# Capsule routing rounds 2 to 6 as one stream: norms in six pieces inside the stream, softmax per 16 places, at least one chunk per bucket

## The chip, the cores and the metric

The kernel runs on one core of one Trainium2 chip. The metric is the device time of one execution in microseconds. The core has five engines that run beside each other and wait for each other through semaphores: TensorE (PE, matmuls; PEld is its weight load), VectorE (DVE), ScalarE (ACT), GpSimd (POOL) and SyncE (SP), which here only issues DMAs. The host's work is not in the time.

## What is computed

A residual network of four graph layers over 6250 nodes with 128 features and 106250 edges, each followed by a layer norm. The change is in the fourth layer, a routing over capsules: a node's 128 features are 8 capsules of 16. The reference, cut to that layer:

```python
def _L3_gnn_ref(x, edge_index):
    K, NITER, TAU, EPS = 8, 6, 1.0, 1e-12
    def _factor_normalize(v):
        nrm = jnp.linalg.norm(v, axis=-1, keepdims=True)
        return v / jnp.maximum(nrm, EPS)
    n, d = x.shape
    k, dd = (K, d // K)
    src, trg = (edge_index[0], edge_index[1])
    xk = _factor_normalize(x.reshape(n, k, dd))
    z = xk[src]
    u = xk
    for _ in range(NITER):
        p = jax.nn.softmax(jnp.sum(z * u[trg], axis=2) / TAU, axis=1)
        msg = (z * p[:, :, None]).reshape(-1, d)
        agg = jax.ops.segment_sum(msg, trg, num_segments=n)
        u = _factor_normalize(agg.reshape(n, k, dd) + xk)
    return u.reshape(n, d)
...
x = _layernorm(x + _L3_gnn_ref(x, edge_index), axis=-1)
```

The edges hold both directions of 50000 drawn pairs and one self loop per node. The edge list is an input, so the order of the work for it is made on the chip.

## The kernel before

Nodes lie in 49 tiles of 128 (NT; NTP = 50 with a spare one). The edges are sorted by the tile of their target, a bucket, and each bucket is cut into chunks of 128 edges, one edge per partition. Two chunks of one bucket make a pair. The program has room for 464 pairs (NPAIR); a table, pair_tile, tells each pair's bucket at run time, and pair_at where its data lie in DRAM. A bucket's last pair may have an empty half, which the flags in pair_ok set to zero.

The first round (`first_round`) gathers z for each edge with indirect DMAs and stores it in zo_tab, beside the bytes of two 128 x 128 selection matrices per chunk. Rounds 2 to 6 are `later_rounds` (L2177), called once with 5 rounds. Each round goes over 116 groups (NO) of four pairs, which are eight chunks or "places" (OC). For a group g:

- SP loads four pairs of zo_tab, 192 KB each, into one of six slots (L2258), once the message and the selection matrix that used the slot are done.
- ACT turns bytes into float matrices: `widen` (wide, L2389) and `hot` (hots, L2401), two buffers each.
- PE, `expand` (L2437): eight matmuls bring u of the target nodes to the edges, into PSUM.
- DVE, `product` (L2299): z times that, into prod, of which there is one buffer. POOL, `fold` (L2276): adds the upper half of each capsule's 16 products to the lower. DVE, `reduce` (L2306): sums the rest, which gives dot.
- ACT, `exponential` (L2396). DVE: `total_share` (L2310), `share_inverse` (L2315), `flagged` (L2320), `shares` (L2327), 8 places at a time.
- POOL, `message` (L2268): z times share. PE, `total` (L2449): eight matmuls sum the edges of a pair into their nodes, in PSUM. DVE, `add` (L2338): four adds, one per pair, into the bucket's tile of the sums.

The order of each engine's instructions is written out by hand. DVE works on step k: reduce(k), add of group k - 2, product(k + 1), and the other three adds between the small share operations. POOL does message(k - 1) and then fold(k + 1). PE does expand(k + 2) and total(k - 1). Most engines take four groups of bucket numbers at a time into registers (`registers`).

At a round's end all waits for all. ACT squares the sums in four parts (L2425), when the last add is done; DVE sums the squares (L2373); ACT takes roots in two parts (L2428), which needs another table of functions (ACT_TABLE_LOAD); DVE bounds them from below (L2376), inverts them (L2377) and multiplies (L2378), and s_go tells PE and ACT that the next round may begin. The sums alternate between two arrays (sums_of); ACT resets the idle one to the unit vectors of x in ten parts during the next round (L2406). x itself stays in x_sb throughout, for the residual addition behind the rounds (L2480).

## Time and profile before

| | |
|---|---|
| median of the timed runs | 9093.38 us (3 runs, 9089.47 to 9102.39) |
| span of the profiled execution | 9046.9 us |
| median less span | 46.5 us |
| busy PE, PEld | 5679.9 us (63%), 4627.8 us (51%) |
| busy DVE, POOL, ACT | 5810.5 us (64%), 6454.7 us (71%), 2292.8 us (25%) |
| rounds 2 to 6 | from about 6749 to 8990 us of the span |

The span is from the first to the last instruction of one execution under the hardware profiler. The page gives no separate device time for that execution; what lies around the span is taken as the difference to the median. Busy time of an engine counts its instructions, not its waits. Matmuls are pipelined and their ends are modelled: two blocks of eight matmuls can show 1.95 us each and start 1.79 us apart. A float32 matmul leaves two records, so a block of eight shows as x16. Lines (L2299) are those of the kernel before.

### The profile page before, as it was taken

The numbers are of one execution on the slowest core, as the hardware profiler recorded it, in microseconds if no ns is written. First come the engines' busy times: TensorE is split into PE (matmuls) and PEld (weight loads), VectorE is DVE, ScalarE is ACT, GpSimd is POOL, SyncE is SP. The second block draws the span as 40 slices with busy tenths as digits, with TensorE's granted clock in tenths as the row PEclk, the third lists the DMA queues.
The fourth block names the chain that finished last, engine by engine and source line by source line (L and its number), as shares of the span: only waits on it lengthen the run. The fifth ranks groups of instructions, "written<-read, shape, count | busy, mean of one in ns | idle before, by whom it ended". The sixth has DMA issues, their size and how long they took to land. (4 is left out here: it accounts for less than half of the span.)

```text
span 9046.9 us, 131904 instructions
## 1 busy us (share of the span) xinstructions
PE 5679.9 (63%) x35786; PEld 4627.8 (51%) x35874; DVE 5810.5 (64%) x15100; ACT 2292.8 (25%) x3456; POOL 6454.7 (71%) x5675
## 2 busy tenths in 40 slices
PE   0990024444488887698344442555559898989896
PEld 0440023333333333566333332555549898989896
DVE  9660035555577666556444446555559898989898
ACT  2000000000100000343222222222226565656564
POOL 4777767777377776674677772777758787878785
PEclk6995555555655555899666666887769999999998
DMA  1780035555599999895333342444457676767674
GB/s 40 289 308 2 2 84 131 131 131 131 101 213 211 210 210 183 263 290 168 88 82 81 80 73 67 128 129 128 130 118 221 191 221 189 219 190 222 190 221 142
DMA packets 1122974, 1403.89 MB, mean 155 GB/s; under 512 B 276858, under 2 KB 948302, under 8 KB 1109198
## 3 DMA queue, kind: packets, MB, share of 16 engines
q1 hardware_dynamic: 968942, 1098.82, 40.7%
q0 software_dynamic: 153312, 296.65, 17.0%
q8 instruction: 309, 5.06, 0.2%
q14 instruction: 411, 3.37, 0.1%
HBM read 1010.93 MB, written 383.96 MB: 154 GB/s over the span
## 5 line engine op out<-in xcount | busy, mean ns | idle before, releaser
L2437 PE MATMUL ps<-u,wide_r 128*128 x9280 | 1140.5, 277 | 129.3 <-issue 88.6
L2268 POOL TENSOR_TENSOR msg_r<-zo_r,share_r 128x1024 f32<-128x1024 f32 x580 | 1123.1, 1936 | 101.7 <-DVE share_r L2327 46.1
L2437 PEld LDWEIGHTS ps<-u,wide_r 128*128 128x128 f32 x9280 | 1092.2, 193 | 131.3 <-issue 131.2
L2449 PE MATMUL ps<-msg_r,hots_r 128*128 128x128 f32 x9280 | 1140.7, 276 | 24.4 <-POOL msg_r L2268 23.1
L2010 POOL DMA_INDIRECT z_r<-x_tab,src_row x880 | 854.4, 971 | 417.2 <-issue 268.0
L2449 PEld LDWEIGHTS ps<-msg_r,hots_r 128*128 128x128 f32 x9280 | 1081.8, 192 | 32.9 <-POOL msg_r L2268 31.9
L297 POOL DMA_INDIRECT rec_tab<-pay,row_i x831 | 808.0, 972 | 374.9 <-issue 275.1
L575 POOL DMA_INDIRECT ring<-y_tab,y_row x880 | 838.0, 952 | 306.9 <-issue 266.0
L1172 POOL DMA_INDIRECT ring_m<-t_tab,src_row x880 | 835.3, 949 | 307.9 <-issue 280.8
L1624 POOL DMA_INDIRECT ring_e<-t_tab,src_row x880 | 832.4, 946 | 271.7 <-issue 268.0
L2276 POOL TENSOR_TENSOR prod_r<-prod_r 128x512 f32<-128x512 f32 x580 | 735.0, 1267 | 319.2 <-DVE prod_r L2299 302.9
L777 PE MATMUL ps<-ring,hots 128*128 128x129 f32 x1760 | 453.2, 438 | 694.8 <-issue 594.9
L1205 DVE TENSOR_REDUCE high_m<-ps 128x4 f32<-128x512 f32 x880 | 605.9, 690 | 344.5 <-PE ps L1260 311.1
L777 PEld LDWEIGHTS ps<-ring,hots 128*128 128x128 f32 x1760 | 394.1, 329 | 754.0 <-issue 688.5
L2152 PE MATMUL ps<-unit,wide_r 128*128 x1760 | 387.2, 410 | 615.1 <-ACT wide_r L2117 615.1
L2338 DVE TENSOR_TENSOR u_sum<-ps,u_sum 128x128 f32 x2320 | 671.9, 290 | 102.6 <-PE ps L2449 20.6
L2299 DVE TENSOR_TENSOR prod_r<-ps,zo_r 128x1024 f32<-128x1024 f32 x580 | 705.3, 1216 | 33.9 <-PE ps L2437 30.9
L2152 PEld LDWEIGHTS ps<-unit,wide_r 128*128 128x128 f32 x1760 | 358.6, 311 | 635.4 <-issue 635.4
L2389 ACT ACTIVATE wide_r<-zo_r 128x1024 f32<-128x1024 uint8 x580 | 605.6, 1044 | 105.8 <-PE ps L2437 62.1
L2401 ACT ACTIVATE hots_r<-zo_r 128x1024 f32<-128x1024 uint8 x580 | 603.5, 1041 | 0.0
L762 DVE TENSOR_TENSOR acc<-ps,acc 128x129 f32 x880 | 258.7, 294 | 507.6 <-PE ps L777 410.6
L1034 ACT ACT_TABLE_LOAD x1 | 1.3, 1283 | 2274.0 <-PEq L107 2274.0
(303 smaller groups left out, 10622.4 us busy)
## 6 DMA issues: line engine op xcount, KB each, us to landing
zo_r<-zo_tab SPq DMA_DIRECT2D x2320, 192.0 KB, 2.8
ring_e<-k_tab SPq DMA_DIRECT2D x464, 260.0 KB
k_tab<-ring_m SPq DMA_DIRECT2D x220, 520.0 KB, 6.3
y_tab<-wide SPq DMA_DIRECT2D x100, 1024.0 KB, 3.9
zo_tab<-z_r SPq DMA_DIRECT2D x110, 512.0 KB, 3.6
hot_bytes_e<-hb_tab SPq DMA_DIRECT2D x464, 64.0 KB, 3.3
dl_b<-dl_tab SPq DMA_DIRECT2D x220, 128.0 KB, 3.8
zo_tab<-hot_bytes SPq DMA_DIRECT2D x220, 128.0 KB
```

The source lines that it names most:

```text
L297: nc.gpsimd.indirect_dma_start(out=rec_tab, out_offset=bass.IndirectOffsetOnAxis(ap=row_i[:, j:j + 1], axis=0), in_=pay[:, j, :], in_offse ...
L575: nc.gpsimd.indirect_dma_start(out=ring[:, s, c, 0:width], out_offset=None, in_=table, in_offset=bass.IndirectOffsetOnAxis(ap=rows[:, q * ...
L777: last = nc.tensor.matmul(sum_of(s, c), hots[:, s, c, :], ring[:, s, c, :], start=True, stop=True)
L1172: nc.gpsimd.indirect_dma_start(out=ring[:, s, c, :], out_offset=None, in_=t_tab, in_offset=bass.IndirectOffsetOnAxis(ap=src_row[:, q * CQ ...
L1624: nc.gpsimd.indirect_dma_start(out=ring[:, b % ZR, c, :], out_offset=None, in_=t_tab, in_offset=bass.IndirectOffsetOnAxis(ap=src_row[:, b ...
L2010: nc.gpsimd.indirect_dma_start(out=z[:, g % ZR, c, :], out_offset=None, in_=x3_tab, in_offset=bass.IndirectOffsetOnAxis(ap=src_row[:, g * ...
L2152: last = nc.tensor.matmul(ps[:, 2 * (g % 2) + c // 4, c % 4 * D:(c % 4 + 1) * D], wide[:, g % WR, c, :], unit[:, bass.ds(tiles[at // CQ, a ...
L2268: nc.gpsimd.tensor_tensor(msg[:, g % WR].rearrange("p c (k d) -> p c k d", d=CD), z_of(g).rearrange("p c (k d) -> p c k d", d=CD), share[: ...
L2276: nc.gpsimd.tensor_tensor(prod[:, :, 0:CD // 2], prod[:, :, 0:CD // 2], prod[:, :, CD // 2:CD], ALU.add).then_inc(s_half, 1)
L2299: v.tensor_tensor(prod[:].rearrange("p (c k) d -> p c (k d)", k=CAPS), up, z_of(g), ALU.mult).then_inc(s_prod, 1)
L2437: last = nc.tensor.matmul(ps[:, 2 * (g % 2) + c // 4, c % 4 * D:(c % 4 + 1) * D], wide[:, g % WR, c, :], u[:, bass.ds(tiles[g % NO % 4 * O ...
L2449: last = nc.tensor.matmul(ps[:, 4 + g % 2, c // 2 * D:(c // 2 + 1) * D], hots[:, g % WR, c, :], msg[:, g % WR, c, :], start=c % 2 == 0, st ...
```

## The change

It does five things.

- The barrier between rounds goes. The groups of all five rounds are one stream of 580, taken in couples q of two groups (290). The norms are made in six pieces of eight tiles (the last has ten), and each piece has its place in the stream: at the first couple after which, by the smallest possible number of pairs for the buckets behind it, its buckets must be complete (`LASTS`, `piece_at`). Roots and units are made for two pieces at once, one couple after the second of them (`couple_at`). PE waits for one more piece of units at every second group at the start of a round.
- The softmax works on 16 places: one exponential, total, inverse, flag product and share per couple. dot, ex, share and tot are twice as wide. prod has two buffers.
- The order of each engine's instructions is new (below).
- x_sb lends its memory to wide, msg and prod. So x is stored to x_kept in DRAM before the first round, and SP loads it back during the last round, into the array of sums that is free by then; the residual addition reads it there. The slots for pairs grow from six to eight.
- Each bucket has at least one chunk, where the counts are made.

```diff
-                    link(v.tensor_scalar(nch_f[:], run[:], float(P - 1), None, ALU.add))
+                    link(v.tensor_scalar(nch_f[:], run[:], float(P - 1), float(P), ALU.add, ALU.max))
...
                     def _(sp):
+                        sp.dma_start(x_kept.rearrange("(t p) d -> p t d", p=P), x_sb[:]).then_inc(s_o, 16)
                         sp.wait_ge(s_u, 1)
                         sp.dma_start(x3_tab.rearrange("(t p) d -> p t d", p=P), unit[:]).then_inc(s_o, 16)
-                        sp.wait_ge(s_o, 16)
+                        sp.wait_ge(s_o, 32)
...
+                NS = NO // 2
-                ZR, WR = 6, 2
-                parts = [(0, 13), (13, 26), (26, 38), (38, NTP)]
+                ZR, WR = 8, 2
+                pieces = [(0, 8), (8, 16), (16, 24), (24, 32), (32, 40), (40, NTP)]
+                NP_R = len(pieces)
+                LASTS = [(NPAIR - NT + min(b, NT) - 1) // OP for _, b in pieces]
+                T = rounds * NO
+                TS = rounds * NS
...
+                    def piece_at(q):
+                        for p, g in enumerate(LASTS):
+                            r, o = divmod(q - (g + 3) // 2, NS)
+                            if o == 0 and 0 <= r < rounds:
+                                return r, p
+                        return None
+
+                    def couple_at(q):
+                        at = piece_at(q - 1)
+                        return (at[0], at[1] // 2) if at and at[1] % 2 else None
...
+                                if g == T - NO // 2:
+                                    sp.wait_ge(s_go, NP_R * (rounds - 1))
+                                    sp.dma_start(sums_of(rounds - 2)[:], x_kept.rearrange("(t p) d -> p t d", p=P))\
+                                      .then_inc(s_x, 16)
...
                         def _(pool):
...
-                            for r in range(rounds):
-                                for k in range(-1, NO + 1):
-                                    if k >= 1:
-                                        message(r * NO + k - 1)
-                                    if k + 1 < NO:
-                                        fold(r * NO + k + 1)
+                            for q in range(-1, TS):
+                                for h in range(2):
+                                    if q + 1 < TS:
+                                        fold(2 * q + 2 + h)
+                                    if q >= 0:
+                                        message(2 * q + h)
...
                         def _(dve):
...
+                            for q in range(-1, TS + 3):
+                                now, ahead = 0 <= q < TS, q + 1 < TS
+                                old, late = 2 * q - 3, 2 * q - 2
+                                behind = 0 <= old < T
+                                if now:
+                                    reduce(2 * q)
+                                if behind:
+                                    add(old, 0)
+                                    add(old, 1)
+                                if now:
+                                    reduce(2 * q + 1)
+                                if behind:
+                                    add(old, 2)
+                                    add(old, 3)
+                                if ahead:
+                                    product(2 * q + 2)
+                                if q % 2 == 1 and q // 2 * 4 < T:
+                                    tiles_in(q // 2)
+                                for n, step in enumerate((total_share, share_inverse, flagged, shares)):
+                                    if now:
+                                        step(q)
+                                    if 0 <= late < T:
+                                        add(late, n)
+                                if ahead:
+                                    product(2 * q + 3)
+                                if piece_at(q):
+                                    square_sums(*piece_at(q))
+                                if couple_at(q):
+                                    units(*couple_at(q))
...
                         def _(act):
...
+                            def square(r, p):
+                                a, b = pieces[p]
+                                act.wait_ge(s_acc, OP * (r * NO + LASTS[p] + 1))
+                                nc.scalar.activation(u[:, a:b, :], sums_of(r)[:, a:b, :], ACT.Square).then_inc(s_sq, 1)
+
+                            def roots(r, j):
+                                a, b = pieces[2 * j][0], pieces[2 * j + 1][1]
+                                act.wait_ge(s_ss, NP_R * r + 2 * j + 2)
+                                nc.scalar.activation(norms(a, b), norms(a, b), ACT.Sqrt).then_inc(s_rt, 1)
+                                act.preload_act_table(ACT.Exp)
...
+                            for q in range(TS + 3):
+                                if q < TS:
+                                    r, o = divmod(q, NS)
+                                    exponential(q)
+                                if couple_at(q):
+                                    roots(*couple_at(q))
+                                if q < TS:
+                                    if 2 * q + 4 < T:
+                                        widen(2 * q + 4)
+                                    hot(2 * q)
+                                    if 2 * q + 5 < T:
+                                        widen(2 * q + 5)
+                                    hot(2 * q + 1)
...
+                                if piece_at(q):
+                                    square(*piece_at(q))
...
                         def _(pe):
...
+                                if r >= 1 and o % 2 == 0 and o // 2 < NP_R:
+                                    pe.wait_ge(s_go, NP_R * (r - 1) + o // 2 + 1)
...
+                            for q in range(-1, TS + 1):
+                                for h in range(2):
+                                    if q + 1 < TS:
+                                        expand(2 * q + 2 + h)
+                                    if q >= 1:
+                                        total(2 * q - 2 + h)
...
-                        link(nc.vector.tensor_tensor(x_sb[:], x_sb[:], u[:], ALU.add))
+                        link(nc.vector.tensor_tensor(x_sb[:], u_sums[(ROUTINGS - 2) % 2][:], u[:], ALU.add))
```

## Rows read from the trace of the kernel before

**Rows 1.** A stretch: us, busy (x) per engine, PEclk, DMA share, GB/s.
```profile
6770.00:7160.00 390.00, 389.88 (x3482) 389.57 (x3481) 370.40 (x1088) 242.44 (x337) 348.33 (x218) 1.00 0.73 221
```

**Rows 2.** Groups by line: xcount | busy us, mean ns | idle before, releaser.
```profile
L2268 POOL TENSOR_TENSOR msg_r<-zo_r,share_r 128x1024 f32<-128x1024 f32 x580 | 1123.1, 1936 | 101.7 <-DVE share_r L2327 46.1
L2276 POOL TENSOR_TENSOR prod_r<-prod_r 128x512 f32<-128x512 f32 x580 | 735.0, 1267 | 319.2 <-DVE prod_r L2299 302.9
L2338 DVE TENSOR_TENSOR u_sum<-ps,u_sum 128x128 f32 x2320 | 671.9, 290 | 102.6 <-PE ps L2449 20.6
L2299 DVE TENSOR_TENSOR prod_r<-ps,zo_r 128x1024 f32<-128x1024 f32 x580 | 705.3, 1216 | 33.9 <-PE ps L2437 30.9
L2389 ACT ACTIVATE wide_r<-zo_r 128x1024 f32<-128x1024 uint8 x580 | 605.6, 1044 | 105.8 <-PE ps L2437 62.1
...
L2306 DVE TENSOR_REDUCE dot_r<-prod_r 128x64 f32<-128x512 f32 x580 | 396.5, 684 | 13.8 <-POOL prod_r L2276 13.4 <-issue 0.4
L2327 DVE TENSOR_TENSOR share_r<-ps,ex_r 128x64 f32<-128x64 f32 x580 | 130.5, 225 | 20.4
```

**Rows 3.** Timeline inside a round: start us, us, engine, line, operation, [idle before].
```profile
7293.47 1.21 DVE L2299 TENSOR_TENSOR prod_r<-ps,zo_r 128x1024 f32<-128x1024 f32 x1
7294.68 0.29 DVE L2338 TENSOR_TENSOR u_sum<-ps,u_sum 128x128 f32 x1
7294.74 1.95 PE L2449 MATMUL ps<-msg_r,hots_r 128*128 128x128 f32 x16
...
7295.96 0.23 DVE L2327 TENSOR_TENSOR share_r<-ps,ex_r 128x64 f32<-128x64 f32 x1
...
7296.26 1.93 POOL L2268 TENSOR_TENSOR msg_r<-zo_r,share_r 128x1024 f32<-128x1024 f32 x1 [0.22 <-DVE share_r L2327]
...
7296.53 1.95 PE L2437 MATMUL ps<-u,wide_r 128*128 x16
```

**Rows 4.** Timeline, early in the second of these rounds.
```profile
7204.83 1.27 POOL L2276 TENSOR_TENSOR prod_r<-prod_r 128x512 f32<-128x512 f32 x1 [2.16 <-DVE prod_r L2299]
...
7206.05 1.93 POOL L2268 TENSOR_TENSOR msg_r<-zo_r,share_r 128x1024 f32<-128x1024 f32 x1
7206.13 0.69 DVE L2306 TENSOR_REDUCE dot_r<-prod_r 128x64 f32<-128x512 f32 x1 [0.55 <-POOL prod_r L2276]
```

**Rows 5.** Timeline over the end of the first of these rounds.
```profile
7160.78 1.95 PE L2437 MATMUL ps<-u,wide_r 128*128 x16
...
7174.47 1.59 DVE L2338 TENSOR_TENSOR u_sum<-ps,u_sum 128x128 f32 x4 [0.77 <-PE ps L2449]
7176.09 5.82 ACT L2425 ACTIVATE u<-u_sum 128x1664 f32<-128x1664 f32 x4 [6.71 <-DVE u_sum L2338]
7177.78 7.00 DVE L2373 TENSOR_REDUCE nrm<-u 128x104 f32<-128x1664 f32 x4 [1.72 <-ACT u L2425]
7181.92 1.28 ACT L2428 ACT_TABLE_LOAD   x1
...
7184.99 1.45 DVE L2377 RECIPROCAL nrm<-nrm 128x208 f32<-128x208 f32 x1
7186.48 3.62 DVE L2378 TENSOR_TENSOR u<-u_sum,nrm 128x3328 f32<-128x3328 f32 x1
...
7196.50 7.13 PE L2437 MATMUL ps<-u,wide_r 128*128 x48 [22.18 <-issue]
```

**Rows 6.** Two stretches behind that round end; columns as in rows 1.
```profile
7196.00:7198.00 2.00, 1.50 (x7) 1.51 (x8) 0.00 (x0) 0.00 (x0) 0.00 (x0) 0.50 0.00 0
7200.00:7202.00 2.00, 2.00 (x20) 2.00 (x19) 1.22 (x1) 1.85 (x2) 0.59 (x1) 1.00 0.00 0
```

**Rows 7.** Line L2437 (ns min/median/max, first and last start), and the last multiply.
```profile
L2437 PE MATMUL ps<-u,wide_r x9280: 274/275/577, 6748.9 to 8957.5; 128*128 x198
...
8986.70 3.36 DVE L2378 TENSOR_TENSOR u<-u_sum,nrm 128x3072 f32<-128x3072 f32 x1
```

**Rows 8.** The stretch of the transfer of unit to DRAM; columns as in rows 1.
```profile
5552.00:5564.00 12.00, 0.00 (x0) 0.00 (x0) 0.01 (x1) 0.00 (x0) 0.00 (x0) 0.50 0.90 264
```

More of the change, by code:

```diff
@@ L2249, in _ @@
                         def _(sp):
-                            for g in range(rounds * NO):
+                            for g in range(T):
                                 o = g % NO
@@ L2291, in _, with tiles_in @@
                             link(v.tensor_copy(flat[:, 512:2 * NPAIR], ok[:, 512:2 * NPAIR]))
+                            sets = {}
+                            def tiles_in(b):
+                                sets.pop(b - 2, None)
+                                sets[b] = registers(DVE_ENGINE, pair_tile, b * 4 % NO, NT)
                             def product(g):
@@ new lines, in square_sums, with units @@
+                            def square_sums(r, p):
+                                a, b = pieces[p]
+                                dve.wait_ge(s_sq, NP_R * r + p + 1)
+                                v.tensor_reduce(norms(a, b), capsules(u, a, b), AX.X, ALU.add).then_inc(s_ss, 1)
+                            def units(r, j):
+                                a, b = pieces[2 * j][0], pieces[2 * j + 1][1]
+                                dve.wait_ge(s_rt, NP_R // 2 * r + j + 1)
+                                link(v.tensor_scalar(norms(a, b), norms(a, b), 1e-12, None, ALU.max))
+                                link(v.reciprocal(norms(a, b), norms(a, b)))
+                                for a, b in pieces[2 * j:2 * j + 2]:
@@ new lines, in _ @@
+                            for g in range(4):
+                                widen(g)
+                            for q in range(TS + 3):
[11 more added lines that the diff above has]
+                                    hot(2 * q + 1)
+                                    if 4 <= o < 4 + RESETS and r + 1 < rounds:
+                                        if o == 4 and r >= 1:
+                                            act.wait_ge(s_go, NP_R * r)
+                                        reset(r, o - 4)
+                                if piece_at(q):
+                                    square(*piece_at(q))
```

189 lines of the change are left out of this document (71 added, 118 removed).

## The prediction

> **What bounds the kernel now.** I read the page first. VectorE (DVE), GpSimd (POOL) and TensorE (PE) are each busy for 60 to 70% of the span, so shares don't decide, and the work has many stages. The change touches one of them, routing rounds 2 to 6. It begins with the first expansion at 6748.9 and ends with the last unit vectors at 8986.7 + 3.4 = 8990.1 us [rows 7]: 2241.2 us.
>
> Next I read the stage by stretches. Between two round ends PE is busy for 389.9 of 390 us at full clock, DVE for 370, POOL for 348 [rows 1]. The timeline shows the same: an expansion or a total starts 1.79 us after the one before it [rows 3], and a group (4 pairs, 8 places) has one of each, so at least 3.57 us. From the first expansion of the stage to the last of its first round (7160.78) [rows 5] are 115 groups in 411.9 us, 3.58 each, 7.16 for two groups. So PE is the bound inside a round, by little: the longest loop beside it is not far away.
>
> At a round's end PE stands still. Its first matmul of the next round starts at 7196.50, 35.7 us after the last expansion of the round [rows 5], 32.1 more than the usual 3.6. The rows between show the reason: last adds, squares over everything, square sums, the table load for the roots, roots, reciprocals, multiplies, one behind the other. There are four such ends between rounds and one at the stage's end.
>
> **The change, part by part.** I write q for a couple of groups (2q, 2q+1), S(q) for the start of its share instruction on DVE, and count from there.
>
> *Softmax per 16 places.* Four small DVE operations are saved per two groups, each about 0.21 us from start to start (six instructions from the add at 7294.68 to the share at 7295.96) [rows 3]. The four that stay are twice as wide, the widest longer by 0.07 us. DVE's load falls by some 0.6 us per couple (4 x 0.21 less what the wider ones add). PE was the bound, so this brings nothing by itself. What counts is the new order of waits. Both groups of a couple now need both dot products before one share instruction, and POOL's order is fold(2q+2), message(2q), fold(2q+3), message(2q+1). So fold(2q+3) stands behind message(2q), which waits for share(q); and share(q+1) needs reduce(2q+3), which needs that fold. Queued behind this reduce on DVE are two adds, the next product and the small operations. This is a loop over one couple. Its terms:
> - share, 128 values: 0.29 (225 ns with 64 values, 290 ns for an add of 128) [rows 2]; passed to POOL: 0.07 (7296.19 to 7296.26) [rows 3]
> - message: 1.94 less the overlap of 0.04 that two POOL operations show (fold 7204.83 + 1.27, message at 7206.05) [rows 4]: 1.90
> - fold(2q+3): 1.27, and 0.03 until the reduce starts [rows 4]: 1.30
> - reduce(2q+3): 0.68, the next may start a little before it ends: 0.63
> - two adds in a row: 0.43 (four take 1.59, so 1.59 - 0.29 = 1.30 for three starts) [rows 5] + 0.21
> - product: 1.21 from start to start [rows 3], some are shorter: 1.17
> - total, add, inverse, add, flag, add, to the next share: six starts, 1.28 in [rows 3] with narrower operations; 1.27
>
> Sum 7.27 us per couple, against 7.16 now. Bounds: 7.15, where PE holds as today, and 7.36 if every start distance takes its upper value. I take 7.27, since nearly each term has its own row. PE would then wait about 0.1 us per couple for a message. 289 couples from S(0) to S(289): 2101 us. POOL itself needs 2 x (1.94 + 1.27) = 6.4 us and is not the bound, but sits in the loop.
>
> *Norms in six pieces inside the stream.* In an ordinary step DVE runs a last add and product(2q+3) until 1.6, then reduce(2q+2) and two adds until 2.8, then waits for fold(2q+3) until 3.6. The norm work is put behind product(2q+3), so a step is longer by (end of its norm work - 1.6 - 0.8). The work, from the rows of a round's end [rows 5]: square of a piece 1.0 us on ScalarE (ACT) (5.82 for 6400 values; 1024 here), square sums 1.12 (7.00 for 6400), units of two pieces 0.25 + 0.95 + 2 x 1.12 + passing = 3.5 (reciprocal 1.45 for 208 values, 128 here; multiply 3.62 for 3328). The square isn't ready when DVE comes: ACT issues it last in its step, after hot(2q+1), which needs total(2q-1); widen and hot take 1.04 each [rows 2]. So square sums start at 2.7, not 1.6. Where a couple has roots, ACT first does two table loads of 1.28 and a root, 2.9 together, ahead of two widens and two hots, and the square of that step is ready at about 5.0 only. Steps of one round's end, with the end of their norm work and what they cost: piece 0, 3.9, 1.5; piece 1, 3.4, 1.1; piece 2 and units 0-1, 5.0 + 1.1 + 3.6 = 9.7, 7.3; piece 3, 4.5, 2.1 (its hot waits for a total that was late, since PE's first expansion of the new round waits for unit 0 until 8.7); piece 4 and units 2-3, 9.8, 7.4; piece 5 (1280 values), 5.2, 2.8; units 4-5, 5.7, 3.3. Sum 25.5 us. The loop has no slack to give this back. So an end costs 25.5 instead of 32.1, and the stall moves from PE's one wait into DVE's waits for ACT and PE's waits for units: four ends 102. Last round: its first three steps cost 9.9, and from the last S about 21 us follow (messages, totals, adds of 4 x 0.43, squares and sums of three pieces, two roots with table loads, two sets of units). From the first expansion to S(0) about 12 us (E, product, fold, reduce, exponential, small ones, with PE at half clock).
>
> *PE's clock.* In the new steps with units PE stands idle for 5 to 8 us. Before the first matmuls of a round (22 us idle) the granted clock is 0.50, 1.2 GHz, and reaches 1.00 about 4 us later [rows 6]. Full effect would be 1.8 us per such step, twice per end, 14 us in all; none if the clock holds through 8 us. I take 8.
>
> *Keeping x in DRAM.* The store of 3.2 MB runs beside the first norm; the like transfer of unit keeps the queues 0.90 busy at 264 GB/s over 12 us [rows 8], and there are more than 20 us of vector work ahead of the wait: nothing (else up to 12). The load back comes in mid round on SyncE (SP)'s queue, ahead of pair loads that already take 221 GB/s, 0.73 of the engines [rows 1]. They wait some 11 to 12 us behind it; eight slots lead by 4 us or so over what is needed: 7 us once, 0 to 12.
>
> *At least one chunk per bucket* changes no count here: a bucket has its 106 or 128 self loops and thousands of edges. Resets, registers and the last addition move, with their cover (0.72 us copies on an ACT with over 2 us free): nothing.
>
> **Sum.** 12 + 2101 + 102 + 10 + 21 = 2246, + 8 + 7 = 2261 against 2241: +20 us. The profiled span is 9046.9 us, the median of the timed runs 9093.4; the 46.5 around the span are carried over: 9113.
>
> **A rule of the skill.** The row: a multiply of units with both inputs in SBUF, 3.62 us for 3328 values, runs with POOL idle [rows 5]; no row shows it beside a POOL operation. The Trainium skill, page "SBUF — State Buffer", section "SBUF: two separate sides", says that a DVE operation with two SBUF inputs and a GpSimd operation that reads SBUF exclude each other for their whole length. No trace here shows that yet. By that rule units 4-5 would meet a message; the rival below has the price.
>
> **Rivals.**
> - *DVE is relieved and PE keeps its pace* (15%): starts are tighter than I add up, the loop is under 7.16. For it: DVE's load does fall, and PE's floor of 7.15 is only 0.12 away. Against it: the loop's terms are mostly POOL's two operations, which don't shrink. 289 x 0.11 = 32 less: 9081.
> - *The ends vanish too* (10%): squares are ready in time, only DVE's own 17 us of norm work less 7 x 0.8 of slack stays, 12 per end instead of 27.5: 62 less than that, 9019.
> - *The loop is longer* (17%), on the slow side: same mechanism at the upper starts, 7.36, decided at DVE's product and adds between POOL's fold and the next share; it is slower than now from 7.20 on, with the other terms as they are: + 26, 9139.
> - *Multiply and message exclude each other* (6%): one message of 1.94 per end and multiply, four or five times: +8, 9121.
> - *The rounds don't overlap* (7%): the first expansion waits for units that wait for the last adds, an end costs 32 as today: + 18, 9131.
> - *As forecast* (45%): 9113, by itself 9085 to 9140.
>
> **How the numbers follow.** About 0.2% (18 us) is what a measurement of this kernel can tell from no change, so the bounds are 9075 and 9112. My forecast stands at the upper one and splits: 0.22 slower, 0.21 same, 0.02 faster. The slow rivals give 0.26 slower, 0.04 same; relieved DVE 0.12 faster, 0.03 same; vanished ends 0.10 faster. Together 0.24, 0.28, 0.48. For 8 in 10, the range takes in 9085 to 9140, the relieved DVE, half of the way to the vanished ends, and the longer loop with some hold from the rest: 9035 to 9160.
>
> **What would show it.** Inside a round: share to share 7.2 to 7.35 us; PE's busy share under 100% with waits for messages; reduce of the odd group waiting for POOL's fold. At an end: gaps on DVE ahead of the square sums, released by ACT, and PE waiting for unit multiplies at the first and fifth group; first expansion to first expansion about 58 x 7.27 + 28 = 449 us, nearly the 447.6 of now (6748.9 to 7196.5). In the last round: one stretch in which widen waits for its pair load. Wrong if PE still runs at 7.15 per couple, if POOL's fold doesn't release the reduce, or if a round takes under 440 us.

## The result, and the profile after

The changed kernel takes 9120.06 us (median of 6 runs, 9115.39 to 9132.35); the kernel before, beside it on the same chip, 9094.90 us (6 runs, 9089.47 to 9102.39). The ratio is 1.0030, with a 95% interval of 1.0018 to 1.0041: slower by some 25 us, where 9113 was forecast against 9093.4, +20.

The profiled execution of the changed kernel took 9115.39 us with a span of 9113.6. Rounds 2 to 6 run from the first expansion at 6792.8 to the end of the last unit vectors, 9054.12 + 2.63 = 9056.75: 2264.0 us, against 2241.2 before [rows 7]. The forecast had 2261.

In the changed kernel wide, msg and prod lie in the memory of x_sb, and the profile calls them all x_sb. Its lines: expand L2502, total L2514, message L2297, fold L2305, product L2333, reduce L2341, share L2363, add L2377, square sums L2383, bound from below L2388, reciprocal L2389, multiply L2391, widen L2432, hot L2445, square L2456, root L2461 and the table load after it L2462.

A stretch inside the first of these rounds answers to [rows 1] (us, busy and count of PE, PEld, DVE, ACT and POOL, clock, DMA share, GB/s):

```profile
6820.00:7160.00 340.00, 339.98 (x3037) 339.79 (x3036) 290.92 (x757) 205.39 (x248) 299.02 (x190) 1.00 0.72 221
```

DVE's share has fallen from 95% to 86%, as the saved small operations say, and PE is still busy throughout. The groups by line in the same stretch answer to [rows 2] (count, busy us, mean ns, idle before and who ended it):

```profile
L2297 POOL TENSOR_TENSOR x_sb<-zo_r,share_r 128x1024 f32<-128x1024 f32 x95 | 183.8, 1934 | 9.6 <-DVE share_r L2363 9.6
L2305 POOL TENSOR_TENSOR x_sb<-x_sb 128x512 f32<-128x512 f32 x95 | 120.0, 1263 | 31.4 <-DVE x_sb L2333 31.4
L2341 DVE TENSOR_REDUCE dot_r<-x_sb 128x64 f32<-128x512 f32 x95 | 64.6, 680 | 31.6 <-POOL x_sb L2305 31.6
```

Durations are what they were. New is that reduce waits for POOL's fold: 31.6 us in 340, where before it was 13.4 us over the whole stage [rows 2]. This is the loop that the prediction describes. The timeline of one couple shows it:

```profile
7291.37 0.28 DVE L2363 TENSOR_TENSOR share_r<-ps,ex_r 128x128 f32<-128x128 f32 x1
7291.72 1.94 POOL L2297 TENSOR_TENSOR x_sb<-zo_r,share_r 128x1024 f32<-128x1024 f32 x1 [0.19 <-DVE share_r L2363]
7293.62 1.27 POOL L2305 TENSOR_TENSOR x_sb<-x_sb 128x512 f32<-128x512 f32 x1
7294.92 0.69 DVE L2341 TENSOR_REDUCE dot_r<-x_sb 128x64 f32<-128x512 f32 x1 [0.40 <-POOL x_sb L2305]
7295.52 0.71 DVE L2377 TENSOR_TENSOR u_sum<-ps,u_sum 128x128 f32 x2
7296.15 1.21 DVE L2333 TENSOR_TENSOR x_sb<-ps,zo_r 128x1024 f32<-128x1024 f32 x1
7297.28 0.27 DVE L2346 TENSOR_REDUCE tot_r<-ex_r 128x16 f32<-128x128 f32 x1
7298.54 0.28 DVE L2363 TENSOR_TENSOR share_r<-ps,ex_r 128x128 f32<-128x128 f32 x1
```

From share to share: 0.35 + 1.90 + 1.30 + 0.60 + 0.63 + 1.13 + 1.26 = 7.17 us. PE's blocks in the same stretch start 1.787 us apart, four of them 7.15 us. So the loop and PE are tied.

The stage's waits (engine, tile and line, who ended it: total us, times, longest) name the rest:

```profile
DVE dot_r L2341 <- POOL x_sb L2305: 165.2, 258, 1.7
PE ps L2502 <- DVE u L2391: 99.4, 12, 9.1
...
DVE nrm L2383 <- ACT u L2456: 58.9, 26, 3.6
```

PE waits for unit vectors three times at each of the four round ends, and DVE's square sums wait for ACT's squares.

The distance from share to share, over all 289 of them, splits the 2231.5 us between the first share (6803.60) and the last (9035.08):

| part | forecast | measured |
|---|---|---|
| first expansion to first share | 12 | 10.8 |
| 289 ordinary couples | 2101 (7.27 each) | 2080 (mean 7.198, median 7.17) |
| four round ends, over that | 102, and 8 for the clock | 136.7 (35.2, 32.8, 35.2, 33.4) |
| first steps of the last round's end | 10 | 9.4 |
| wait at the reload of x | 7 | 5.0 (steps of 11.54 and 7.85) |
| last share to the end | 21 | 21.7 |
| stage | 2261 | 2264 |

So the sum is right by two errors of opposite sign: the loop 21 us too long, the round ends 27 too short.

Beside the kernel before, the 23 us of the stage split like this: there two groups inside a round took 7.16 us and a round end 32.1 over that [rows 5]; here a couple takes 7.198 in the mean (289 x 0.035 = 10 us) and a round end 34.2 (4 x 2.1 = 8 us), and the wait at the reload, 5 us, is new.

The first round end, step by step, in us over an ordinary couple (its seven distances are 9.23, 7.77, 16.75, 10.40, 16.88, 10.82 and 13.79; 7.2 is taken from each):

| step | forecast | measured |
|---|---|---|
| piece 0 | 1.5 | 2.0 |
| piece 1 | 1.1 | 0.6 |
| piece 2, units 0-1 | 7.3 | 9.6 |
| piece 3 | 2.1 | 3.2 |
| piece 4, units 2-3 | 7.4 | 9.7 |
| piece 5 | 2.8 | 3.6 |
| units 4-5 | 3.3 | 6.6 |
| sum | 25.5 | 35.2 |

The timeline of the third step shows where the 9.6 come from:

```profile
7208.37 0.28 DVE L2363 TENSOR_TENSOR share_r<-ps,ex_r 128x128 f32<-128x128 f32 x1
7213.58 1.22 DVE L2383 TENSOR_REDUCE nrm<-u 128x64 f32<-128x1024 f32 x1 [3.57 <-ACT u L2456]
7214.72 0.22 DVE L2388 TENSOR_SCALAR nrm<-nrm 128x128 f32<-128x128 f32 x1
7215.96 2.36 DVE L2391 TENSOR_TENSOR u<-u_sum,nrm 128x1024 f32<-128x1024 f32 x2
7217.32 3.78 PE L2502 MATMUL ps<-u,x_sb 128*128 x16 [8.75 <-DVE u L2391]
7218.24 0.68 DVE L2341 TENSOR_REDUCE dot_r<-x_sb 128x64 f32<-128x512 f32 x1
7221.19 1.23 DVE L2333 TENSOR_TENSOR x_sb<-ps,zo_r 128x1024 f32<-128x1024 f32 x1 [0.42 <-PE ps L2502]
7224.04 0.29 DVE L2377 TENSOR_TENSOR u_sum<-ps,u_sum 128x128 f32 x1 [1.40 <-PE ps L2514]
```

The norm work ends 7218.24 - 7208.37 = 9.87 us behind the share; the prediction had 9.7. What it missed comes after: the expansion that waited for the units takes 3.78 us and not 1.95, and DVE then waits 0.42 and 1.40 us for PE. The stretches show the clock (columns as above):

```profile
7205.00:7210.00 5.00, 3.57 (x32) 3.38 (x31) 4.80 (x13) 4.48 (x6) 3.55 (x3) 1.00 0.82 251
7210.00:7214.00 4.00, 0.00 (x0) 0.00 (x0) 0.43 (x2) 3.55 (x4) 3.75 (x3) 0.86 0.53 159
7214.00:7218.00 4.00, 0.68 (x3) 0.68 (x4) 3.93 (x5) 0.00 (x0) 0.00 (x0) 0.50 0.75 245
7218.00:7222.00 4.00, 4.00 (x21) 4.00 (x21) 3.29 (x8) 1.11 (x2) 0.00 (x0) 0.50 0.06 19
7222.00:7226.00 4.00, 4.00 (x33) 4.00 (x33) 2.40 (x10) 1.53 (x3) 1.78 (x2) 0.86 0.00 0
```

PE works at half clock (0.50, 1.2 GHz) for four microseconds and more after its wait. The other two such expansions of this end, at 7244.47 and 7269.84, take 3.77 and 3.78 us too. Over all twelve of the four round ends the expansion takes 3.45 to 3.78 us and the total behind it 1.95 to 3.08.

The last step has a second cause:

```profile
7263.58 1.93 POOL L2297 TENSOR_TENSOR x_sb<-zo_r,share_r 128x1024 f32<-128x1024 f32 x1 [0.20 <-DVE share_r L2363]
7264.78 0.81 DVE L2388 TENSOR_SCALAR nrm<-nrm 128x144 f32<-128x144 f32 x1
7266.68 1.93 POOL L2297 TENSOR_TENSOR x_sb<-zo_r,share_r 128x1024 f32<-128x1024 f32 x1
7266.72 4.37 DVE L2391 TENSOR_TENSOR u<-u_sum,nrm 128x1024 f32<-128x1024 f32 x2
```

The bound from below takes 0.81 us where it took 0.22 above (0.23 for the same 144 values at the stage's end), and ends at 7265.59, just behind the message (7265.51). The two multiplies (the second has 1280 values, so 2.63 us as at the stage's end) take 4.37, and the message that began 0.04 us before them ends at 7268.61. Together this is 0.6 + 1.7 = 2.3 us, and it is the same at all four round ends. The Trainium skill, page "SBUF — State Buffer", section "SBUF: two separate sides", says that a DVE operation with two SBUF inputs and a GpSimd operation that reads SBUF exclude each other. The multiply has two such inputs, and the trace agrees: 4.37 us for 2.63. The bound from below has only one; that it is held up as well is what its row shows.

### The profile page after: what moved, and what is told of

It is laid out like the page before. It is cut to its first block and busy times, and to the rows that moved or that the text cites. A ratio compares the mean times of both kernels' runs of the same rounds, so it can differ in the third digit from the quotient of the medians.

```text
span 9113.6 us, 130034 instructions
## 1 busy us (share of the span) xinstructions
PE 5746.7 (63%) x35874; PEld 4658.2 (51%) x35874; DVE 5636.6 (62%) x13980; ACT 2308.9 (25%) x3203; POOL 6422.3 (70%) x5675
## 5 line engine op out<-in xcount | busy, mean ns | idle before, releaser
L2502 PE MATMUL ps<-u,x_sb 128*128 x9280 | 1156.2, 279 | 139.3 <-DVE u L2391 99.4
L2297 POOL TENSOR_TENSOR x_sb<-zo_r,share_r 128x1024 f32<-128x1024 f32 x580 | 1122.2, 1935 | 85.8 <-DVE share_r L2363 85.8
L2502 PEld LDWEIGHTS ps<-u,x_sb 128*128 128x128 f32 x9280 | 1105.5, 196 | 142.3 <-issue 142.3
L2514 PE MATMUL ps<-x_sb,hots_r 128*128 128x128 f32 x9280 | 1149.3, 278 | 24.8 <-DVE u_sum L2377 15.8
L2514 PEld LDWEIGHTS ps<-x_sb,hots_r 128*128 128x128 f32 x9280 | 1095.2, 194 | 31.1 <-issue 18.4
L2305 POOL TENSOR_TENSOR x_sb<-x_sb 128x512 f32<-128x512 f32 x580 | 733.0, 1264 | 390.7 <-DVE x_sb L2333 390.7
L2377 DVE TENSOR_TENSOR u_sum<-ps,u_sum 128x128 f32 x2320 | 666.4, 287 | 118.8 <-PE ps L2514 11.4
L2333 DVE TENSOR_TENSOR x_sb<-ps,zo_r 128x1024 f32<-128x1024 f32 x580 | 703.9, 1214 | 18.8 <-PE ps L2502 14.5
L2445 ACT ACTIVATE hots_r<-zo_r 128x1024 f32<-128x1024 uint8 x580 | 609.0, 1050 | 197.9 <-PE ps L2514 196.7
L2432 ACT ACTIVATE x_sb<-zo_r 128x1024 f32<-128x1024 uint8 x580 | 606.7, 1046 | 123.3 <-PE ps L2502 91.7
```

What stands on the lines that cost most here:

```text
L2297: nc.gpsimd.tensor_tensor(msg[:, g % WR].rearrange("p c (k d) -> p c k d", d=CD), z_of(g).rearrange("p c (k d) -> p c k d", d=CD), share[: ...
L2305: nc.gpsimd.tensor_tensor(prod[:, g % 2, :, 0:CD // 2], prod[:, g % 2, :, 0:CD // 2], prod[:, g % 2, :, CD // 2:CD], ALU.add).then_inc(s_h ...
L2333: v.tensor_tensor(prod[:, g % 2].rearrange("p (c k) d -> p c (k d)", k=CAPS), up, z_of(g), ALU.mult).then_inc(s_prod, 1)
L2502: last = nc.tensor.matmul(ps[:, 2 * (g % 2) + c // 4, c % 4 * D:(c % 4 + 1) * D], wide[:, g % WR, c, :], u[:, bass.ds(sets[g // 4][g % 4 * ...
L2514: last = nc.tensor.matmul(ps[:, 4 + g % 2, c // 2 * D:(c // 2 + 1) * D], hots[:, g % WR, c, :], msg[:, g % WR, c, :], start=c % 2 == 0, st ...
```

## The experiments

The kernel before runs beside each. Chips differ by up to 57 us, so a time is read as a ratio to the kernel before on the same chip; the changed kernel's is 1.0030. The first four runs share a chip on which the kernel before takes 9100.27 us (20 runs), so the changed kernel would take some 9128 there; their expected times were told from its 9120 and are some 8 us low for that chip. From the traces comes "the stretch", the time from the first share to the last, 2231.5 us in the changed kernel. The ratios are:

| run | ratio, 95% interval | the stretch |
|---|---|---|
| e1 squares early | 0.9964 (0.9950 to 0.9978) | 2180.9 |
| e2 warm | 1.0004 (0.9994 to 1.0013) | 2210.7 |
| e3 no norms | 0.9853 (0.9837 to 0.9870) | 2084.9 |
| e4 third add ahead | 1.0020 (1.0010 to 1.0029) | 2224.5 |
| e5 dummy in the loop | 1.0040 (1.0025 to 1.0054) | 2256.1 |
| e6 dummy off the loop | 1.0023 (1.0014 to 1.0033) | 2229.0 |
| e7 early and warm | 0.9945 (0.9928 to 0.9962) | 2164.5 |
| e8 e7, and x in eight pieces | 0.9938 (0.9922 to 0.9955) | 2160.2 |
| e9 the changed kernel again | 1.0027 (1.0018 to 1.0037) | 2236.7 |
| e10 e8, and the third add ahead | 0.9919 (0.9906 to 0.9933) | 2139.1 |

**Without the norms.** This kernel leaves out all norm work of rounds 2 to 6 (squares, sums, roots, units, and the waits on them; the reload of x waits for the adds instead), so its rounds go on from the first round's unit vectors.

```diff
-                                if piece_at(q):
-                                    square_sums(*piece_at(q))
-                                if couple_at(q):
-                                    units(*couple_at(q))
...
-                                if r >= 1 and o % 2 == 0 and o // 2 < NP_R:
-                                    pe.wait_ge(s_go, NP_R * (r - 1) + o // 2 + 1)
```

> The changed kernel without norms in rounds 2 to 6: no squares, square sums, roots or multiplies to units and no waits for them, so u stays that of round 1 throughout; all else is in place. It measures what the norms cost in the stream. By the trace of the changed kernel, couples apart from round ends take 7.14 to 7.17 us, so 289 couples take 2066 to 2072, and the stage 2110 us in place of 2264: 150 to 155 us less, 8965 to 8970. If the cost of the norms were hidden as meant, the difference would be under 70 us (DVE's own 17 us per round less its slack).

Measured: 8963.63 us (ratio 0.9853), stretch 2084.9, that is 146.6 us less. The round ends and the last steps of the table above make 136.7 + 9.4 = 146.1. So the split by distances is right: the ends cost what they show, and what stays is the loop, with a mean of 7.197 us per couple, and the one wait at the reload (11.38 and 7.92).

**Squares early.** ACT does a piece's square right behind the exponential (and the roots, where there are some), ahead of the casts of that couple.

```diff
                                 if couple_at(q):
                                     roots(*couple_at(q))
+                                if piece_at(q):
+                                    square(*piece_at(q))
                                 if q < TS:
...
-                                if piece_at(q):
-                                    square(*piece_at(q))
```

> One edit to the changed kernel: ScalarE squares a piece right behind the exponential (and roots) of the couple, ahead of its two widens and two hots, not behind them. Theory A (at a round's end DVE stands at the square sums because ScalarE issues the square last; in the changed kernel's trace DVE waits 63.5 us in all for u, 3.6 us at most): nearly all of that goes, steps with a piece get shorter by what they waited (3.57 us in the steps with roots, 1.1 to 2.8 in others), about 12 us per round end, 45 to 55 us in all: 9065 to 9075 us. Theory B (PE's wait for the units and its half clock set the round's end, the squares are hidden behind them): under 10 us less, 9110 to 9120. What would be late next: the roots in the same steps and PE's first expansion at half clock.

Measured: 9070.08 us (5 runs, 9060.45 to 9075.53; ratio 0.9964), stretch 50.6 us shorter. DVE's waits for ACT's squares are gone from the list of waits, and the first end's steps are 7.90, 7.53, 13.42, 7.76, 13.14, 7.98 and 14.41, 21.7 us over the ordinary ones where it was 35.2; in the mean of the four ends it is 22.0 where it was 34.2. ACT's order in the step with roots is now

```profile
7216.52 0.31 ACT L2439 ACTIVATE ex_r<-dot_r 128x128 f32<-128x128 f32 x1 [2.41 <-DVE dot_r L2341]
7216.85 1.28 ACT L2461 ACT_TABLE_LOAD   x1
7218.15 0.31 ACT L2461 ACTIVATE nrm<-nrm 128x128 f32<-128x128 f32 x1
7218.47 1.28 ACT L2462 ACT_TABLE_LOAD   x1
7219.77 1.06 ACT L2456 ACTIVATE u<-u_sum 128x1024 f32<-128x1024 f32 x1
7220.73 1.04 ACT L2432 ACTIVATE x_sb<-zo_r 128x1024 f32<-128x1024 uint8 x1
```

Before this edit the square stood behind two casts and two selection casts, 3.8 us later. So 12 of an end's 34 us came from one line's place in ACT's order. With it the change is faster than the kernel before.

**Throwaway matmuls.** At groups 0, 4 and 8 of a round, 24 matmuls into a PSUM buffer that is overwritten next, ahead of the wait for the units.

```diff
-                                if r >= 1 and o % 2 == 0 and o // 2 < NP_R:
-                                    pe.wait_ge(s_go, NP_R * (r - 1) + o // 2 + 1)
                                 pe.wait_ge(s_wide, g + 1)
                                 if g >= 2:
                                     pe.wait_ge(s_prod, g - 1)
+                                if r >= 1 and o in (0, 4, 8):
+                                    for i in range(24):
+                                        nc.tensor.matmul(ps[:, 2 * (g % 2) + i % 2, 0:D], wide[:, g % WR, i % OC, :],
+                                                         wide[:, g % WR, 0, :], start=True, stop=True)
+                                if r >= 1 and o % 2 == 0 and o // 2 < NP_R:
+                                    pe.wait_ge(s_go, NP_R * (r - 1) + o // 2 + 1)
```

> One edit to the changed kernel: where PE waits for units at groups 0, 4 and 8 of a round, it first does 24 matmuls whose result is overwritten. They last 5.4 us at full clock and use a selection matrix on itself. Theory A (the half clock after 8 us of idle costs about 2 us in each of the three steps with units: share to share 16.75 and 16.88 us where a count at full clock gives 14.5 to 14.7): granted clock stays near 1.00 there, the expansion behind the wait takes 1.95 us and not 3.78, 3 x 2 us less per end, 24 us less in all: 9096. Theory B (the stall is DVE's own chain, PE catches up): under 5 us less, 9115 to 9120. If the 24 matmuls outlast the wait, it gets slower by their rest, up to 5 us each.

Measured: 9102.37 us (ratio 1.0004), stretch 20.8 us shorter; the third step of the first end is 14.71 instead of 16.75, the last 12.65 instead of 13.79. The first expansion runs at full clock:

```profile
7219.46 5.62 PE L2501 MATMUL ps<-x_sb 128*128 128x128 f32 x48 [1.27 <-ACT x_sb L2432]
7226.97 2.05 PE L2506 MATMUL ps<-u,x_sb 128*128 x16 [1.88 <-DVE u L2391]
```

and so does the stretch around it:

```profile
7226.00:7230.00 4.00, 3.04 (x27) 3.04 (x28) 3.83 (x7) 0.19 (x1) 0.00 (x0) 1.00 0.38 135
```

The half clock's price in the changed kernel is thus at least 20.8 / 4 = 5.2 us per end (one of the twelve expansions behind units still takes 2.97 us here); the forecast had 2.

**A dummy inside the loop and outside it.** Both kernels add the same store of zeros to a 128 x 128 tile on DVE, once per couple. In the first it stands ahead of product(2q+2), in the second behind product(2q+3).

```diff
+                                if q >= 0:
+                                    dve.wait_ge(s_pad, q + 1)
+                                v.memset(pad[:], 0.0).then_inc(s_pad, 1)
                                 if ahead:
                                     product(2 * q + 2)
```

> A dummy store of zeros to a 128x128 tile (about 0.2 us of DVE) stands in every couple behind reduce(2q+1) and the adds, ahead of product(2q+2), inside the chain share, message, fold, reduce, adds, product, share. Theory A (this chain is a bound of the ordinary couples, tied with TensorE's four back-to-back steps of 1.787 us): the couple goes from 7.17 to about 7.35 us; over some 255 ordinary couples of 289 that is +45 us beside the changed kernel, about 9160 to 9170 us. Rival B (TensorE's 7.15 us alone sets the pace, the chain has slack): the dummy is hidden and the time stays within 5 us of the changed kernel's, about 9115 to 9125.

> The same dummy store of about 0.2 us stands once per couple behind product(2q+3) instead, where DVE waits some 0.4 us for the fold of the next couple. Theory A: it is outside the chain and fills idle time, so ordinary couples stay at 7.17 us and the time within 10 us of the changed kernel's, about 9115 to 9130. Rival B (DVE's total work sets the pace, wherever it lies): about 0.2 us per couple, +45 us, as in the run with the dummy inside the chain.

Measured: 9077.67 us inside (5 runs from 9075.10), 9062.20 outside (10 runs up to 9069.19), on one chip. The timelines, the inside one first:

```profile
7292.86 0.17 DVE L2413 MEMSET pad_r<- 128x128 f32 x1
7292.94 1.16 DVE L2335 TENSOR_TENSOR x_sb<-ps,zo_r 128x1024 f32<-128x1024 f32 x1
...
7300.11 0.17 DVE L2413 MEMSET pad_r<- 128x128 f32 x1
7300.19 1.16 DVE L2335 TENSOR_TENSOR x_sb<-ps,zo_r 128x1024 f32<-128x1024 f32 x1
```

```profile
7290.67 0.17 DVE L2424 MEMSET pad_r<- 128x128 f32 x1
7290.75 0.63 DVE L2343 TENSOR_REDUCE dot_r<-x_sb 128x64 f32<-128x512 f32 x1
```

The size was wrong: the store takes 0.17 us, but what stands behind it starts 0.08 us after it, so it costs 0.08 and not 0.2. Inside the loop that is what the couple grows by (7292.94 to 7300.19 are 7.25, median 7.26 against 7.17), and the stretch by 24.6 us. Outside it the median couple is 7.18 and the stretch 2.5 us shorter than in the changed kernel (the ordinary couples are unchanged, 7.199 us in the mean; the ends are 3 us shorter). The same work costs 27 us of the stretch in one place and nothing in the other, so the loop is a bound. By the times alone the two differ by 15.5 us with ranges that don't meet; beside the changed kernel's ratio (1.0030) the times of neither settle anything. The profiled execution of the inside one took 9089.37 us, 11.7 above its median; whether some of that lies in the stretch isn't known, so the 7.26 us of the couple are the firmer number.

**Third add ahead.** One of the adds between the small share operations moves ahead of reduce(2q+1), where DVE waits for the fold.

```diff
                                     add(old, 1)
+                                    add(old, 2)
                                 if now:
                                     reduce(2 * q + 1)
                                 if behind:
-                                    add(old, 2)
                                     add(old, 3)
```

> One edit to the changed kernel: on DVE a third add of the old group goes ahead of the reduce that waits for POOL's fold, where DVE idles 0.4 us, so the loop share, message, fold, reduce, adds, product, share is shorter by about 0.4 us, 6.8 in place of 7.17. Theory A (the loop and PE's floor of 4 x 1.787 = 7.15 us are tied, so PE sets the pace once the loop is shorter): couples take 7.15, 0 to 8 us less in all: 9112 to 9120. Theory B (my forecast's: the loop alone sets the pace): 0.3 us and more per couple, over 60 us less: 9050.

Measured: 9117.13 us (ratio 1.0020), stretch 7.0 us shorter. The median couple is 7.15 us, PE's four blocks. The loop can't be seen any more and PE is the bound; a rival in which only DVE's total work counts has nothing for this, since the work is the same. The mean falls further, from 7.198 to 7.142: in the changed kernel 17 couples take 7.5 us (in two of them an add on DVE starts 0.34 and 0.51 us late; the others weren't traced back) and nothing makes up for them. Here only 6 do, and 16 couples take 6.7 to 7.0 us, where the changed kernel has one. Right behind each of the 6 stands a short one, as 7.50 and then 6.80 us, together two ordinary ones: late couples are caught up. Against this the first two steps of each end grow, to 10.4 and 8.6 us from 8.9 and 8.1, and eat half of it.

**Both repairs, and x in pieces.** Squares early and twelve throwaway matmuls; then also the reload of x as eight transfers, one every four groups.

```diff
-                                if g == T - NO // 2:
-                                    sp.wait_ge(s_go, NP_R * (rounds - 1))
+                                if g >= T - NO // 2 and (g - T + NO // 2) % 4 == 0 and (g - T + NO // 2) // 4 < 8:
+                                    k = (g - T + NO // 2) // 4
+                                    a, b = k * NTP // 8, (k + 1) * NTP // 8
...
```

> Both repairs at once: the squares stand ahead of the casts on ACT, and twelve throwaway matmuls run where TensorE waits for the units at groups 0, 4 and 8 of a round. Theory A (the half clock still costs after the squares are early): a further 8 to 16 us off the time with early squares alone (9070), about 9055 to 9062 us. Rival B (with the squares early, TensorE's wait of 6 us no longer lowers the clock, or the throwaway matmuls only delay the useful ones): 9070 or up to 10 us more.

> As the kernel with both repairs, and the store x is read back in eight pieces of a few tiles, one every four groups, instead of in one transfer at the middle of the last round. Theory A (the one gap of about 5 us at couple 261, 11.4 and 7.9 us instead of twice 7.15, is the pair loads standing behind that transfer): 4 to 5 us less than the kernel with both repairs, about 9050 to 9058 us. Rival B (the same bytes take the same engines' time wherever they lie, since the DMA engines are already busy for .73 of the stretch): no change beside the kernel with both repairs.

Measured: 8995.20 and 8991.07 us beside 9042.80 for the kernel before on that chip (ratios 0.9945 and 0.9938), stretches of 2164.5 and 2160.2. The expected times were told for another chip and can't be compared; the ratio of e7 is 0.0019 under that of e1, 17 us, and the stretch 16.5 shorter, at the upper edge of what theory A had. In the first end the profile shows no wait of DVE up to the last set of units, and its own operations are what the end costs:

```profile
7160.19 1.21 DVE L2333 TENSOR_TENSOR x_sb<-ps,zo_r 128x1024 f32<-128x1024 f32 x1
7161.32 1.21 DVE L2383 TENSOR_REDUCE nrm<-u 128x64 f32<-128x1024 f32 x1
7162.44 0.91 DVE L2388 TENSOR_SCALAR nrm<-nrm 128x128 f32<-128x128 f32 x1
7163.39 0.95 DVE L2389 RECIPROCAL nrm<-nrm 128x128 f32<-128x128 f32 x1
7164.38 3.00 DVE L2391 TENSOR_TENSOR u<-u_sum,nrm 128x1024 f32<-128x1024 f32 x2
7167.30 0.68 DVE L2341 TENSOR_REDUCE dot_r<-x_sb 128x64 f32<-128x512 f32 x1
```

An end costs 18 us here (17.8 to 18.4; steps 7.89, 7.53, 12.38, 7.53, 12.41, 7.80 and 13.32 in the first). The exclusion now shows in every set of units of an end: 0.91 for 0.22 us and 3.00 for 2.36 in the first two, and the third as before, together 5.0 us.

Twelve throwaway matmuls don't always keep the clock up. In front of the third set of units of an end PE still waits 2.22 us behind them, and the expansion there takes 2.05 us in two ends of e7 and one of e8, but 2.56 to 3.53 in the others. This one is of e8:

```profile
7202.28 2.94 PE L2505 MATMUL ps<-x_sb 128*128 128x128 f32 x24 [0.49 <-ACT x_sb L2436]
7207.45 3.19 PE L2510 MATMUL ps<-u,x_sb 128*128 x16 [2.22 <-DVE u L2395]
```

The last step of such an end then takes 13.3 us where it is otherwise 12.65. With x in pieces the steps of 11.22 and 7.95 us in the last round are gone from the list (4.8 us); the stretch is 4.3 us shorter, and the times of the two can't be told apart.

**The changed kernel again, and all four edits.**

> The changed kernel as it is, beside the kernel before and the next kernel, so that all three stand on one chip. Theory A: its ratio to the kernel before is again between 1.001 and 1.005, and the stretch from the first share to the last 2231 us within 5. Rival B (the 0.3% was particular to the first chip or to the run): the ratio is under 1.001.

> Early squares, twelve throwaway matmuls at groups 0, 4 and 8, x read back in eight pieces, and the third old add ahead of reduce(2q+1). Theory A (the ordinary couple is tied between the DVE chain and TensorE's four steps of 1.787 us, and the fourth edit takes it from 7.17 to 7.15 us): 4 to 6 us less than the same kernel without the fourth edit, that is a ratio of about 0.993 to the kernel before and 2154 to 2157 us from the first share to the last. Rival B (as in the run with the third add ahead alone, steps 1 and 2 of each round end grow by 1.2 and 0.4 us because DVE has no slack left there, and eat the gain): 2158 to 2164 us, no gain.

Measured, with 9065.06 us for the kernel before: 9089.80 us (ratio 1.0027) and 8994.38 us (0.9919, 0.9906 to 0.9933). The change's 0.3% is the same on a second chip, with a stretch of 2236.7 (5.2 longer than the first, just outside what was expected; 2.6 of it lie in the four round ends and 1.9 at the reload, 12.13 and 9.18). All four edits together are 0.8% faster than the kernel before and 97.6 us shorter in the stretch than the changed kernel beside them. The fourth edit brought 21.1 us over e8, where 4 to 6 were expected: I had multiplied the difference of the medians, 0.02 us, but the mean of the ordinary couples falls from 7.200 to 7.125, since late couples are caught up. And the growth of the first two steps, which rival B had, isn't there (7.77 and 7.53, beside 7.89 and 7.53 in e8): in e4 it came with the late squares.

## Why the prediction was right

**Total and sign.** +20 us were forecast in the stage, +23 measured, +25 in the times. The case "as forecast" (9085 to 9140) held. But the sum held by two terms that failed in opposite directions, 21 us against 27. The sign and the mechanism were forecast; that the size came out to 5 us is luck.

**The loop: mechanism right, size off.** Share, message, fold, reduce, adds, product, small operations: that it decides is shown by the reduce's waits and by the pair of dummies. No term was far off; each was equal or a little above what the timeline shows: share and pass 0.36 for 0.35, message 1.90 and fold 1.30 as measured, reduce 0.63 for 0.60, adds 0.64 for 0.63, product 1.17 for 1.13, small operations 1.27 for 1.26. Together 0.10 us, 289 times, of which late couples take some back. The measured 7.17 lies in the lower part of the 7.15 to 7.36 given, beside PE's own bound: the rival "DVE is relieved and PE keeps its pace" had 32 us less in the loop, and 21 of them came. "PE would wait about 0.1 us per couple" was wrong: PE is busy for 339.98 of 340 us.

**The round ends: the step that failed.** The forecast was 25.5 us and 2 for the clock, 27.5; measured 34.2 in the mean. The DVE side of each step was worked out well (9.87 against 9.7 for the third). Three things made the rest:
- The clock. "I take 8" for all four ends, in two steps each. There are three such steps in an end, and the half clock holds through the expansion and mostly into the total behind it (3.78 and 3.01 us in place of 1.95 each in the first); DVE waits for both. Throwaway matmuls give back 5.2 us per end, so 21 and not 8.
- The exclusion of multiply and message, a rival with 6% and + 8 us. It is there in every run that has norms: 2.3 us per end in the changed kernel. It goes beyond the multiply: the bound from below (tensor_scalar, one input) also waits, 0.81 for 0.22. It was a cost to add to the forecast, not a case against it.
- The remaining 1 to 2 us (34.2 - 25.5 - 5.2 - 2.3 = 1.2) are not settled further.

The square's lateness was forecast in place and size (5.0 behind the share; 7213.55 - 7208.37 = 5.18). What it is worth, 12 us per end, only the run showed. The rival "the ends vanish too" had 12 us per end with squares in time: e7 has 18, so even then the estimate of DVE's own work was short: 5.0 of the 6 us are the exclusion, and in two of the four ends the clock takes 0.7.

**The reload of x:** 7 forecast, 5.0 measured. widen waits for a pair load behind the transfer, once:

```profile
8812.68 1.06 ACT L2432 ACTIVATE x_sb<-zo_r 128x1024 f32<-128x1024 uint8 x1 [8.76 <-DMA zo_r<-zo_tab]
```

**The signs.** Reduce waiting for the fold, DVE's gaps ahead of the square sums and PE's waits at the first and fifth group all show (and one at the ninth, which wasn't named). Share to share is 7.17 in the median where 7.2 to 7.35 was named. From the first expansion of a round to that of the next are 424.5, 453.4, 451.2 and 452.4 us, where 449 was forecast and under 440 was named as wrong. The first alone is under it, and by the place of the mark: its end's long steps fall behind the next round's first expansion, while each later distance holds one whole end.

**The 46.5 us around the span: a wrong reading.** Only 1.8 us lie around the span of the changed kernel (9115.39 - 9113.6). The profiled execution of before was a quick one: its stage began at 6748.9 [rows 7], that of the changed kernel at 6792.8. Little ahead of it was changed, one small operation and a store. The start differs by chip: the first expansion of other runs comes at 6741 to 6746 on the chip where the kernel before takes 9042.8, at 6762 and 6765 where it takes 9065.1, and at 6789 to 6804 where it takes 9100.3. Most of it lies in one stage, the gathers that fill ring_m; its line in before and in after:

```profile
L1172 POOL DMA_INDIRECT ring_m<-t_tab,src_row x880: 943/949/1781, 2454.3 to 3596.0; - x176
```

```profile
L1173 POOL DMA_INDIRECT ring_m<-t_tab,src_row x880: 940/946/1778, 2454.0 to 3639.9; - x176
```

The 44 us went into the offset and so did no harm: the sum was made as a difference. Whether before's profile comes from a quicker chip isn't known; its 6748.9 is what such a chip shows.

**Not tried.** To put the barrier back alone: DVE does the units of a round's last pieces behind products of the next round, so a PE that waited for all pieces would never be released. What the overlap is worth by itself is open. The store of x wasn't tried alone either.

## What to carry to other kernels

A barrier that is taken away gives nothing while the work behind it runs through engines whose queues are in another order: here the barrier's 32 us became 34 in pieces, and moving one square ahead of four casts in ACT's queue made it 22. Where two bounds are tied, give the loop slack before the pace-making engine is counted: late couples are then caught up, and the gain is that of the means, not of the medians. And when a step is moved beside other work, price it there: its clock, the port it shares, and who is queued behind it.

## What the runs showed of the hardware

- TensorE: after waits of 6.8 to 9.1 us the first block of eight matmuls takes 3.45 to 3.78 us and not 1.95, the next 1.95 to 3.08, at clock 0.50 in the stretch read; in e1 the waits are 4.9 to 6.2 us and the first block takes 3.45 to 3.78 as well. With 24 throwaway matmuls in the wait it takes 1.95 or 2.05 us in 11 of 12 cases (2.97 once); with twelve, 1.95 to 2.29 at the first two waits of an end, and at the third up to 3.53 (e7, e8) or always 2.05 (e10).
- VectorE and GpSimd: a tensor_scalar took 0.22 us alone, 0.81 beside GpSimd's multiply (the message) and 0.91 beside its add (the fold, e7), and ends 0.08 us after GpSimd's operation; a pair of multiplies 2.36 and 3.00, or 2.63 and 4.37. Neither shows as a wait: they are longer instructions.
- VectorE: a memset of 128 x 128 shows 0.17 us, but the instruction behind it starts after 0.08.
- ACT: a table load takes 1.28 us, and the root starts 0.02 us behind it; both switches and the root together take 2.9 us.
